# Attention in runs of three: scores three tiles in a row, then the values of three, on TensorE

## The reference

```
q, k = rope(q), rope(k)
s = einsum('bthd,bshd->bhts', q, k) * scale
logits = 2 * log(|s| + 1e-30) + log_G[t] - log_G[s]      # causal
a = exp(logits - max over s)                             # = decay * s**2 / its row maximum
num = einsum('bhts,bshd->bthd', a, v);  den = sum(a)
y = num / (den + 1e-6), then normalised per head and projected
```

## Time and profile before

| | |
|---|---|
| time, median of 3 runs | 2179.81 us (2179.35 to 2181.45) |
| the profiled execution: time, span | 2178.68 us, 2176.9 us |
| mean granted TensorE clock | 0.954 |
| attention: first score matmul, last row maximum | 263.8 us, 1342.9 us |
| busy over the span | PE 92%, DVE 83%, ACT 59%, POOL 36% |

### The profile page before, as it was taken

One profiled execution on the slowest core, in us unless ns is written; L12 is line 12 of the kernel. 1 busy time (PEld: TensorE's weight loads), 2 busy tenths in 40 slices (PEclk: granted clock), 3 DMA queues, 4 the chain that ended last, 5 costly groups with the idle time before them and its releaser, 6 DMA issues. The chain is left out here.

```text
span 2176.9 us, 37910 instructions
## 1 busy us (share of the span) xinstructions
PE 1995.8 (92%) x13199; PEld 1365.7 (63%) x13199; DVE 1803.1 (83%) x2652; ACT 1294.1 (59%) x2168; POOL 781.8 (36%) x729
## 2 busy tenths in 40 slices
PE   7999689999999999999999996899726999999994
PEld 5677434444444444544444443789625999999994
DVE  6999769999999999999999997777587778777783
ACT  4444367777777777777777774344303656566661
POOL 3777501111111111111111111466525666666663
PEclk9999789999999999999999998999956999999997
DMA  5887883235543244543255402344332333444444
GB/s 191 286 275 270 272 203 82 80 101 122 126 120 72 82 112 122 121 104 81 78 126 122 121 20 69 95 134 131 117 107 68 83 71 80 87 86 88 88 85 107
DMA packets 156104, 260.57 MB, mean 120 GB/s; under 512 B 44568, under 2 KB 120160, under 8 KB 149472
## 3 DMA queue, kind: packets, MB, share of 16 engines
q1 hardware_dynamic: 127792, 214.07, 35.3%
q0 software_dynamic: 15840, 22.29, 6.5%
q10 hardware_dynamic: 12304, 22.02, 3.1%
HBM read 162.40 MB, written 100.14 MB: 121 GB/s over the span
## 5 line engine op out<-in xcount | busy, mean ns | idle before, releaser
L980 ACT ACTIVATE att_sb_a<-att_ps_s,att_sb_fg,att_sb_f 128x1024 f32<-128x1024 f32 x384 | 458.7, 1203 | 286.3 <-PE att_ps_s L1117 272.5
L1018 DVE TENSOR_TENSOR keep_sb_store<-keep_sb_store,att_sb_a 128x1024 f32<-128x1024 f32 (+1 forms) x528 | 533.1, 1036 | 34.5 <-ACT att_sb_a L980 32.6
L936 POOL TENSOR_SCALAR_AFFINE_SELECT att_sb_dec<-att_sb_dec 128x128 f32<-128x128 f32 x256 | 130.1, 508 | 941.4 <-ACT att_sb_dec L970 941.4
L1136 PE MATMUL att_ps_off<-att_sb_a,att_sb_v 128*64 128x512 f32 x1520 | 389.0, 601 | 0.1
L1117 PEld LDWEIGHTS att_ps_s<-keep_sb_late,att_sb_k 64*128 64x128 f32 x1920 | 158.4, 185 | 159.0 <-issue 86.7
L1117 PEld LDWEIGHTS att_ps_s<-att_sb_q,att_sb_k 64*128 64x128 f32 x1896 | 157.2, 186 | 160.4 <-issue 89.1
L1769 ACT ACTIVATE ffn_sb_h<-ffn_ps_p,ffn_sb_b_cols 128x256 f32<-128x256 f32 x320 | 151.7, 476 | 169.3 <-PE ffn_ps_p L1960 168.4
L1117 PE MATMUL att_ps_s<-att_sb_q,att_sb_k 64*128 64x512 f32 (+2 forms) x1896 | 243.7, 381 | 3.5 <-DMA att_sb_k<-k_rows 3.5
L1117 PE MATMUL att_ps_s<-keep_sb_late,att_sb_k 64*128 64x512 f32 (+3 forms) x1920 | 246.8, 381 | 0.0
L1034 DVE SCALAR_TENSOR_TENSOR att_sb_a<-att_ps_s,att_sb_dec 128x1024 f32<-128x1024 f32 (+3 forms) x256 | 209.7, 819 | 41.0 <-PE att_ps_s L1117 36.8
L1874 DVE TENSOR_TENSOR ffn_sb_h_lo<-ffn_sb_h,ffn_sb_h_hi 128x256 fp32r<-128x256 f32 x320 | 213.0, 708 | 28.1 <-ACT ffn_sb_h_hi L1762 26.8
(11 more groups left out here) (256 smaller groups left out, 3583.7 us busy)
## 6 DMA issues: line engine op xcount, KB each, us to landing
q_rows<-early_sb_halves SPq DMA_DIRECT2D x32, 1024.0 KB, 4.9
att_sb_k<-k_rows SPq DMA_DIRECT2D x60, 512.0 KB, 15.8
ffn_sb_raw<-L_ffn_W ACTq DMA_DIRECT2D x36, 512.0 KB, 4.0
close_sb_nT<-num_rows SPq DMA_DIRECT2D x34, 512.0 KB, 4.0
k_rows<-early_sb_halves SPq DMA_DIRECT2D x16, 1024.0 KB, 4.9
keep_sb_late<-q_rows SPq DMA_DIRECT2D x32, 512.0 KB, 14.0
num_rows<-att_sb_num SPq DMA_DIRECT2D x64, 256.0 KB, 2.5
att_sb_hb<-half_log SPq DMA_DIRECT2D x15, 1024.0 KB, 22.8
```

The costliest lines, as they stand in the source:

```text
L936: nc.gpsimd.affine_select(out=tile, in_=tile, compare_op=ALU.is_ge, fill=0.0, base=0, pattern=[[1, P]], channel_multiplier=-1).then_inc(de ...
L980: nc.scalar.activation(x, s_ps[slot(op)][:, :, :], ACT.Square, scale=f[:, p, i - 1, s:s + 1], bias=fg[:, p, i - 1, s:s + 1]).then_inc(sq_d ...
L1018: nc.vector.tensor_tensor(x[:, :, c:TB], x[:, :, c:TB], y[:, :, c:TB], ALU.max).then_inc(max_done, 1)
L1136: last = nc.tensor.matmul(ps[h * HD:(h + 1) * HD, c:TB], v_tile, a[:, a_slot(op), h, c:TB], start=(s == 0), stop=(s == (ST * i if kind == ...
```

## The change

PATTERN is another order of the same 44 steps. Values follow every third place instead of every second (GROUP = 3), computed by values_places: the earliest third place at least 2 (off) or 5 (diag) places after the scores, and one group later where a new block would otherwise share a group with the block before it in the same bank. The relative places of the ACT and DVE steps are changed to match, and the waits for the first pair's portions of data hang on the first step that needs each. No instruction of the arithmetic is added or removed.

```diff
-PATTERN = ("o1 d3 o1 d3 x0 o1 d3 o1 d3 "
-           "o2 o2 d1 o2 d1 o2 x3 o2 d1 o2 d1 o2 o2 "
-           "o3 d2 o3 d2 o3 x1 o3 d2 o3 d2 o3 o3 d0 o3 d0 x2 o3 o3 d0 o3 d0 o3")
+PATTERN = ("d3 o1 o1 d3 o1 d3 d3 o1 o2 o2 o2 d1 o2 x0 x3 "
+           "o2 d1 o2 o2 d1 o2 d1 o3 d2 o3 o3 d2 d2 o3 o3 "
+           "d2 d0 o3 x1 o3 o3 o3 o3 d0 d0 x2 d0 o3 o3")
+GROUP, OFF_LAG, DIAG_LAG = 3, 2, 5
+def values_places(place):
+    at = {}
+    for kind, lag in (("off", OFF_LAG), ("diag", DIAG_LAG)):
+        block, last = None, 0
+        for op in sorted((op for op in place if op[1] == kind), key=place.get):
+            d = place[op] + lag
+            d += (GROUP - 1 - d) % GROUP + 0.5
+            if block not in (None, (op[0], op[2])) and d <= last:
+                d = last + GROUP
+            block, last = (op[0], op[2]), max(d, last)
+            at[op] = last
+    return at
     def values_at(op):
-        d = place[op] + (2.5 if op[1] == "off" else 5.5)
-        return d if int(d) % 2 else d + 1
+        return at_values[op]
     def max_at(op):
         if op[1] == "off":
-            return place[op] + 1.8 if op[3] else place[op[:3] + (1,)] + 1.79
-        return place[op] + 4.8
+            return place[op] + 2.25 if op[3] else place[op[:3] + (1,)] + 2.24
+        return place[op] + 4.81
-    sq_order = Order({op: place[op] + (0 if op[1] == "off" else 2.2) for op in offs + diags})
-    dec_order = Order({op: place[op] - 5 for op in diags})
-    et_order = Order({(q, i): place[q, "off", i, 0] + 0.5 for q, i in blocks})
+    sq_order = Order({op: place[op] + (0 if op[1] == "off" else 2.96) for op in offs + diags})
+    dec_order = Order({op: place[op] - 5.95 for op in diags})
+    et_order = Order({(q, i): place[q, "off", i, 0] - 1.18 for q, i in blocks})
-    own_order = Order({op: place[op] + 0.3 for op in diags})
-    row_order = Order({op: place[op] + 0.6 for op in maxes})
+    own_order = Order({op: place[op] + 0.34 for op in diags})
+    row_order = Order({op: place[op] - 0.11 for op in maxes})
-    part_order = Order({(q, i): values_at(last_off(q, i)) + 1.2 for q, i in blocks})
-    total_order = Order({(q, i): values_at(last_own(q, i)) + 1.2 for q, i in owns})
+    part_order = Order({(q, i): values_at(last_off(q, i)) + 0.55 for q, i in blocks})
+    total_order = Order({(q, i): values_at(last_own(q, i)) + 0.29 for q, i in owns})
...
-                if kind == "off" and s == 0:
-                    if q == 0 and i == 1:
-                        pe.wait_ge(first.part_in, FIRST_PART)
-                    elif q == 0 and i == 2:
-                        pe.wait_ge(first.some_in, FIRST_SOME)
-                    elif i == (1 if q else 3):
-                        arrived(pe, q)
+                if q and kind == "off" and i == 1 and s == 0:
+                    arrived(pe, q)
+                if op == first_use[0]:
+                    pe.wait_ge(first.part_in, FIRST_PART)
+                if op == first_use[1]:
+                    pe.wait_ge(first.some_in, FIRST_SOME)
+                if op == first_use[2]:
+                    arrived(pe, 0)
```

More of the change, by code:

```diff
@@ L796, in last_own @@
         return (q, "diag", i, ST - 1)
+    at_values = values_places(place)
     def values_at(op):
-        d = place[op] + (2.5 if op[1] == "off" else 5.5)
-        return d if int(d) % 2 else d + 1
+        return at_values[op]
     def max_at(op):
         if op[1] == "off":
-            return place[op] + 1.8 if op[3] else place[op[:3] + (1,)] + 1.79
-        return place[op] + 4.8
+            return place[op] + 2.25 if op[3] else place[op[:3] + (1,)] + 2.24
+        return place[op] + 4.81
     blocks = [(q, i) for q in range(PAIRS) for i in OFFS]
@@ L820, in attend @@
+    total_order = Order({(q, i): values_at(last_own(q, i)) + 0.29 for q, i in owns})
     slots = Order({op: place[op] for op in offs + diags})
     pe_todo = [(place[op], "s", op) for op in place] + [(values_at(op), "av", op) for op in offs + diags]
[L823 to L826, removed]
+    act_todo = [(place[op] + (0 if op[1] == "off" else 2.96), "sq", op) for op in offs + diags]
@@ L827, in attend @@
+    act_todo += [(place[op] - 5.95, "dec", op) for op in diags]
+    act_todo += [(place[q, "off", i, 0] - 1.18, "et", (q, i)) for q, i in blocks]
+    act_todo += [(q * N + N * 0.88, "factors", (q + 1,)) for q in range(PAIRS - 1)]
     dve_todo = [(max_at(op), "max", op) for op in offs + diags]
-    dve_todo += [(place[op] + 0.3, "own", op) for op in diags]
-    dve_todo += [(place[op] + 0.6, "row", op) for op in maxes]
+    dve_todo += [(place[op] + 0.34, "own", op) for op in diags]
+    dve_todo += [(place[op] - 0.11, "row", op) for op in maxes]
@@ L830, in attend @@
     dve_todo += [(max_at(last_off(q, i)) + 0.01, "scale", (q, i)) for q, i in blocks]
-    dve_todo += [(values_at(last_off(q, i)) + 1.2, "part", (q, i)) for q, i in blocks]
-    dve_todo += [(values_at(last_own(q, i)) + 1.2, "total", (q, i)) for q, i in owns]
+    dve_todo += [(values_at(last_off(q, i)) + 0.55, "part", (q, i)) for q, i in blocks]
+    dve_todo += [(values_at(last_own(q, i)) + 0.29, "total", (q, i)) for q, i in owns]
     pe_todo.sort(), act_todo.sort(), dve_todo.sort()
@@ L1078, in _ @@
         def _(pe):
+            in_part = {(0, "off", 1, s) for s in range(ST)}
+            in_some = {(0, "off", 2, s) for s in range(2 * ST)} | {(0, "diag", 1, s) for s in range(ST)}
+            scored = [op for op in s_order if op[0] == 0 and op[1] != "max"]
+            first_use = [next(op for op in scored if op in in_part), next(op for op in scored if op in in_some),
+                         next(op for op in scored if op not in in_part | in_some)]
+            first_full = next(op for op in av_order if op[0] == 0 and op not in in_part)
             def wait_slot(user):
@@ L1131, in values @@
                     v_tile = first.v_part[:, s, :]
-                elif q == 0 and s == 0 and kind == "off" and i == 2:
+                elif op == first_full:
                     pe.wait_ge(first.v_in, 16)
```

## The result

The changed kernel takes 2129.77 us (median of 4 runs, 2129.44 to 2130.49) against 2180.18 before: ratio 0.9769, interval 0.9752 to 0.9786. Forecast were 2137 and a range of 2124 to 2158. The gain is 50.4 us where the sum in the prediction had 42.5. The profiled execution took 2129.61 us, 49.1 less than the one before.

A forecast was written before the change was run, and what follows sets the result against it. It took the attention to be bound by PE's own work, 12% of it changing between kinds of work. Terms -41.2 - 6 + 2 + 1.6 + 1.1 = -42.5 us gave 2137 us, range 2124 to 2158.

The forecast's parts named there:

- Fewer runs: On PE, score runs fall from 355 to 242 (0.20 us each), values runs from 355 to 231 (0.15): -41.2 us.
- PE's waits in mid-stream: First values of a block wait less for part or total, behind three score tiles instead of two: -6 us.
- late squares: Off tiles in first place of three scores may have their square late for their values: +2 us, at most 16.
- The one wait that I found in the lists: Every third pair a score waits for a transpose's buffer, its row maximum about 0.3 us late: 1.5 us in all.
- Start: First pair: one values tile fewer before the second portion of data, +1.0 us; +1.6 us in the sum.
- End: The last two transposes come together, so two row maxima instead of one stand at the end: +1.1 us.
- the period: Sign in the profile after: a pair's period is 63 us or a little over.
- the three full scores: Sign in PE's timeline: three full scores take 2.27 to 2.28 us.
- DVE's 96%: Sign in the profile after: DVE is busy some 96% of a pair's window.
- DVE as the bound: Rival: DVE takes over, its forced idling keeping the period at 64.8 us; -16 us, 2163; 12% for 2150 to 2175.
- Only part of the price saved: Rival: only part of a run's 0.35 us goes with the run; with a third, -14 us, 2166; 2%.
- Values that wait for squares: Rival: ACT reaches each values run late; at 0.35 us late, +38 us, 2218; 7%.

The follow-up runs named there:

- start: Changed kernel with the first pair's first query factor and o1.2's values put back as before: 2126.91 us against 2129.64 for the changed kernel run again.
- light_rows: Changed kernel with DVE's row maxima reading only 16 of each 128 columns (maxima left incomplete): 2129.52 us against 2129.64, ratio 0.9769 to before.
- g1_new: Changed kernel with values after every place (GROUP = 1 instead of 3): ratio 1.0253 to the kernel before.
- g2_new: Changed kernel with values after every second place (GROUP = 2 instead of 3): ratio 0.9971 to the kernel before.
- g4_new: Changed kernel with values after every fourth place and the diagonal lag 4 instead of 5: ratio 1.012 to the kernel before.
- g3_old: Kernel before with values after every third place only, old order and old relative places kept: ratio 1.0013 to the kernel before.

## Why the prediction was right, and where it was off

The attention's length on PE gives every term; the waits are the length less the work and the price of the runs, pair by pair.

- **Fewer runs, -41.2.** Borne out. The middle score is 0.69, and the price holds from 242 to 509 score runs. One thing was missed: in the new list 11 times two transposes stand side by side, which spares an entry and an exit; such two take 1.90 us instead of 2.04: -1.5.
- **PE's waits in mid-stream, -6, and late squares, +2.** Together -4 forecast. Pairs 1 to 14 waited 13.5 us before and 7.0 after: -6.5 (starts of PE's groups, less 0.69, 0.86 and so on for each and 0.20 and 0.15 for each run). The waits for part and total in these pairs went almost wholly. No off values were seen to wait for their own square, so the +2 was 0. The one wait that I found in the lists is there: o3.11's scores behind the row maximum, 1.8 us in all (forecast 1.5).
- **Start, +1.6.** It is +2.8, from 20.1 to 22.9 us of waits in the first pair, and the run with both causes put back takes 2.7 less. But the two halves are not what was forecast. The second portion of data lets PE go on 23.98 us behind the first score both before and after (263.83 to 287.81, 264.39 to 288.37). The query factor does delay the first values, from 13.15 to 13.86 us behind the first score, but that is swallowed by the wait for the portion: its +0.6 was 0. What costs stands behind the portion: the values of o1.2 take 1.90 us there (289.95 to 291.85) and not 1.0, and PE now waits 0.96 us for part in front of o2.0's values. In the profile of start the portion also came 0.7 us sooner (23.3 us behind the first score), of 2.9 us by which its attention is shorter (1026.6 against 1029.5); whether the edit did that isn't known. PE's timeline after:

```profile
288.37 1.65 PE L1143 MATMUL att_ps_s<-att_sb_q,att_sb_k 64*128 64x512 f32 x6 [4.86 <-DMA att_sb_k<-k_rows]
289.95 1.97 PE L1162 MATMUL att_ps_off<-att_sb_a,keep_sb_store 128*64 128x512 f32 x4
291.85 3.15 PE L1143 MATMUL att_ps_s<-att_sb_q,att_sb_k 64*128 64x512 f32 x18
...
297.87 2.37 PE L1162 MATMUL att_ps_off<-att_sb_a,att_sb_v 128*64 128x512 f32 x10 [0.96 <-DVE att_sb_part L1063]
```

  The granted clock is at or near its lower level (1.2 GHz, 0.50 of 2.4) in these windows of the start (it is the third figure from the end):

```profile
276.00:282.00 6.00, 3.75 (x10) 0.85 (x10) 2.45 (x2) 5.22 (x6) 0.93 (x1) 0.50 1.03 212
...
288.00:294.00 6.00, 5.63 (x22) 2.95 (x24) 0.00 (x0) 1.66 (x2) 0.00 (x0) 0.53 1.08 240
```

  Before, the window from 288 to 294 has 0.72; the next one has 1.00 in both. PE's idle time ahead of the second portion is longer now (4.86 us against 3.48), since one values tile less stands in it, and behind it more of the work runs at the lower level.
- **End, +1.1.** It is -2. The last pair waited 5.8 us before and 3.8 after, and the second row maximum costs nothing outside: the next stage starts 7.46 us behind the last transpose, 7.52 before, and waits for a load until then. The last row maximum begins at 1295.4, where the prediction had 1301. This step was wrong in sign; it looked at the number of steps behind the last values and not at the chain of own, square, values and maxima ahead of them.
- **Sum.** -41.2 - 1.5 - 6.5 + 2.8 - 2.0 = -48.4, against -48.5 of measured length. The rest of the 49.1 lies outside the attention. The forecast of -42.5 is short by 3.1 at the end, 2.5 in the waits and squares and 1.5 in the transposes, and too high by 1.2 at the start. Of the signs that were named for it, the period (62.75 us), the three full scores (2.26) and DVE's 96% came as forecast.
- **The rivals.** DVE as the bound: excluded by light_rows. The Trainium skill ("TensorEngine Tiling (Array Packing)", PSUM Bottleneck) warns that with a faster TensorE the evacuation of PSUM may become the bottleneck. At 96% DVE busy this had not happened. Only part of the price saved: excluded by g1_new and g2_new (60.4 us between them, where a third of the price would be 20.6). Values that wait for squares: not here; g4_new shows the neighbouring wait, of scores for squares, at once.
- **What the prediction didn't say.** It treated the run count as the change and the new places as details. The runs show that with groups of three and either order the gain stands or falls with where part and total are put: without it, 0.1%. That the waits would stay small came out right, since the lists of the changed kernel were gone through for such waits; why the places had been changed was not seen.

## What to carry to other kernels

When an engine is full, look at the distance of starts between groups of one kind and of two: if changing kinds has a price of its own, count the changes in the written-out order, for that is a sum that came out here within some 7% where the waits stayed (5.9 us for 5.5, 60.4 for 61.7). The count alone does not give the time: g3_old has 36.6 us less of changes and no gain. Longer groups make every buffer that is shared between groups come due at another moment, so move the steps that free it (here two short reads of a bank) right behind what they read, ahead of any step that waits for work not yet issued. And look hard at groups longer than the buffers: four scores over three buffers, with places made for three, lost six times what they saved.

## What was not expected of the hardware

Two transposes in a row take 0.93 and 0.97 us where each alone takes 1.02, so there too a change of kind costs something, 0.14 us for an exit and an entry. An engine 96% busy by its record (DVE) gave nothing when 3.8 us of 62.75 were taken from it.
